# A transformer pair on one core: the first feed-forward and the second attention put on one clock of slots

## The reference, cut to what matters

```python
x = x + L0_attn(layernorm(x))   # 8 heads of 64, keys and values from a 64-wide latent
x = x + L0_ffn(layernorm(x))    # ternary weights, 256 -> 1024 -> 1024 -> 1024 -> 256
x = x + L1_attn(layernorm(x))   # 16 heads of 16, rotary, softmax over 1024 keys
x = x + L1_ffn(layernorm(x))    # integer weights, 256 -> 768 -> 256

# L0_ffn, t(x, w, s) = (x @ w.T) * s, w in {-1, 0, 1}
h = silu(t(x, w1, s1)) * t(x, w2, s2)
h = gelu(t(h, h1, hs1)); h = gelu(t(h, h2, hs2)); y = t(h, w3, s3)

# L1_attn
q, k = rope(x @ wq.T), rope(x @ wk.T)
p = softmax(q @ k.T / sqrt(16)); y = (p @ (x @ wv.T)) @ wo.T
```

## Time and profile before

| | us |
|---|---|
| median of the runs (2805.17 to 2809.58) | 2807.38 |
| the profiled execution's time | 2809.22 |
| its span, to which all rows belong | 2807.3 |
| TensorE busy in the span | 2590.9 |
| VectorE busy | 1782.3 |
| ScalarE busy | 1461.3 |
| GpSimd busy | 886.4 |

### The profile page before, as it was taken

One profiled execution on the slowest core, in us unless ns is written; L12 is line 12 of the kernel. 1 busy time (PEld: TensorE's weight loads), 2 busy tenths in 40 slices (PEclk: granted clock), 3 DMA queues, 4 the chain that ended last, 5 costly groups with the idle time before them and its releaser, 6 DMA issues. The chain is left out here.

```text
span 2807.3 us, 35409 instructions
## 1 busy us (share of the span) xinstructions
PE 2590.9 (92%) x13498; PEld 1661.5 (59%) x13498; DVE 1782.3 (63%) x2809; ACT 1461.3 (52%) x1936; POOL 886.4 (32%) x559
## 2 busy tenths in 40 slices
PE   6889889889897999999999949999999999999699
PEld 4444454445444878888888834555555555554488
DVE  6555555565554544555554458887887888787454
ACT  3343343443443446667666614666566566666443
POOL 1545546546554323444343321110010011000144
PEclk8999999999998999999999968999999999999899
DMA  1000000100004300000000043343333333231222
GB/s 52 9 13 22 27 24 23 32 24 24 16 24 126 106 1 23 23 23 23 23 19 5 16 113 68 64 88 59 69 65 58 74 80 62 52 54 18 88 83 76
DMA packets 118284, 129.77 MB, mean 46 GB/s; under 512 B 21216, under 2 KB 92384, under 8 KB 118112
## 3 DMA queue, kind: packets, MB, share of 16 engines
q1 hardware_dynamic: 118112, 127.46, 19.3%
HBM read 92.95 MB, written 33.68 MB: 45 GB/s over the span
## 5 line engine op out<-in xcount | busy, mean ns | idle before, releaser
L1945 DVE TENSOR_REDUCE c_mraw<-c_X 128x1 f32<-128x512 f32 x1024 | 651.3, 684 | 126.8 <-PE c_X L105 118.3
L1867 ACT ACTIVATE c_P<-c_S 128x1024 f32<-128x1024 f32 x512 | 495.8, 1020 | 245.9 <-PE c_S L105 242.2
L105 PE MATMUL c_X<-c_K,c_Q 96*128 96x512 f32 x1024 | 369.0, 443 | 13.4 <-DMA c_Q<-bounce_q 8.6
L488 ACT ACTIVATE a_P<-a_S 128x1024 f32<-128x1024 f32 x256 | 249.0, 1023 | 199.2 <-PE a_S L105 199.2
L105 PEld LDWEIGHTS c_X<-c_K,c_Q 96*128 96x128 f32 x1024 | 181.9, 193 | 267.5 <-issue 197.3
L604 DVE TENSOR_REDUCE a_mraw<-a_X 128x2 f32<-128x1024 f32 x168 | 205.4, 1222 | 147.1 <-PE a_X L105 147.1
L105 PE MATMUL c_S<-c_Q,c_K 98*128 98x512 f32 x1024 | 287.9, 403 | 2.0 <-DMA c_Q<-c_mrow 2.0
L105 PE MATMUL c_O<-c_P,c_V 128*32 128x512 f32 x2048 | 274.4, 608 | 0.2 <-ACT c_P L1867 0.2
L105 PE MATMUL a_O<-a_P,a_V 128*64 128x512 f32 x1024 | 264.2, 640 | 0.0
L1220 POOL TENSOR_TENSOR b_act0l<-b_xf,b_act0h 128x512 fp32r<-128x512 f32 x128 | 169.7, 1327 | 295.8 <-ACT b_act0h L1085 295.8
L733 POOL TENSOR_TENSOR a_accp<-a_accp,a_P 128x1024 f32<-128x1024 f32 x96 | 228.9, 2384 | 67.5 <-ACT a_P L488 58.0
(11 more groups left out here) (310 smaller groups left out, 5377.0 us busy)
## 6 DMA issues: line engine op xcount, KB each, us to landing
c_K<-bounce_k SPq DMA_DIRECT2D x64, 256.0 KB, 7.6
c_Q<-bounce_q SPq DMA_DIRECT2D x128, 128.0 KB, 4.5
b_h_w<-in_L_ffn_h_w SPq DMA_DIRECT2D x16, 512.0 KB, 7.4
bounce_k<-c_comp SPq DMA_DIRECT2D x16, 512.0 KB, 3.2
bounce_q<-c_comp SPq DMA_DIRECT2D x16, 512.0 KB, 3.0
a_rinv<-sums SPq DMA_DIRECT2D x62, 128.0 KB, 2.9
a_ln_x<-in_L_attn_x SPq DMA_DIRECT2D x8, 512.0 KB, 4.7
a_xres<-in_L_attn_x SPq DMA_DIRECT2D x32, 128.0 KB, 2.5
```

What stands on the lines that cost most here:

```text
L105: return pe.eng.matmul(out, lhsT, rhs, start=start, stop=stop, skip_group_check=True)
L488: act.eng.activation(P[n % NP][:, :, :], psS[n % 2][:, :, :], ACT.Exp, scale=SCALE).then_inc(s_exp)
L1867: act.eng.activation(P[n % NP][:, 2 * hp:2 * hp + 2, :], psS[hp][:, :, :], ACT.Exp, scale=SCALE).then_inc(s_exp)
L1945: dve.eng.tensor_reduce(mraw[u % 2][:, at:at + 1], psX[X.slot(key)][:, :], AX.X, ALU.max).then_inc(X.free(key))
```

## The change

`ffn_b` and `attention_c` are taken out and `ffn_attention` is put in their place, one stage of 722 slots (END = 192 + 512 + 18). Slots 0 to 511 are the eight blocks of the feed-forward, 64 slots each; from slot 192 on each slot also holds one half step of the attention (two heads, 128 keys), so that block k + 2 and later runs beside batch k/2. All engines walk through the same slots.

- TensorE in a slot: a pair of scores, a pair of maxima 24 half steps ahead, in even slots the weighing of four heads (two half steps), at most one piece of side work (`x_at`), then 3 products of the feed-forward in even slots and 8 in odd ones.
- Scores and maxima are pairs: two heads on rows 0 to 63 and 64 to 127, three products of halves in 48 rows, the maximum (one part, no longer two) in row 48. One reduction of 1024 columns replaces two of 512. V gets a 17th column of ones at a stride of 16 instead of 16 columns of ones.
- PSUM: one pair of banks for scores, one pair for maxima, one for O, one for all side work (X), two for the feed-forward (Y), where there had been eight for the feed-forward, and three for side work and maxima.
- Weights are not split: every tile is read again from HBM (`wcopy`, 512 KB each, a ring of three) and used as it is. Whether they are exact is found in `attention_a`: 22 times a tile is loaded, copied high by ScalarE, subtracted and reduced by VectorE, and copied from HBM to HBM. If they were not exact, the products would be made in float32.
- The feed-forward's Gelu is made twice by ScalarE, once into the high half and once into float32; before, a copy made the high half.
- Rotation is made by GpSimd in three instructions from a copy by ScalarE; VectorE only shuffles. Values go through HBM like q and k. Each key or query fetch is 6 DMAs instead of 4.
- The host lays out the weights as tiles, and the columns of wv in another order.

`attention_a` (in every unit u from 3 to 24: DMA in turn 2, ScalarE in turn 3, VectorE in turns 0 and 1 of the next unit):

```diff
+    LOWS, LOW_FIRST = 22, 10
+    def tile_at(u, j):
+        n, step = divmod(4 * u + j - LOW_FIRST, 4)
+        return (n, step) if 0 <= n < LOWS else None
 # sync
+            def load_tile(n):
+                sp.wait_ge(s_low, n)
+                sp.eng.dma_start(tile[:, :], wtiles[n]).then_inc(s_tile, 16)
+                sp.eng.dma_start(wcopy[n], wtiles[n]).then_inc(s_copy, 16)
 # scalar, last in a turn
+            def tile_high(n):
+                act.wait_ge(s_tile, 16 * (n + 1))
+                act.wait_ge(s_tile_lo, n)
+                act.eng.activation(tile_hi[:, :], tile[:, :], ACT.Copy).then_inc(s_tile_hi)
 # vector, last in a turn, behind add() and the norm's steps
+            def tile_low(n, step):
+                if step == 2:
+                    dve.wait_ge(s_tile_hi, n + 1)
+                    dve.eng.tensor_tensor(tile[:, :], tile[:, :], f32(tile_hi[:, :]), ALU.subtract).then_inc(s_tile_lo)
+                elif step == 3:
+                    dve.wait_ge(s_tile_lo, n + 1)
+                    dve.eng.tensor_reduce(lows[:, n:n + 1], tile[:, :], AX.X, ALU.max, apply_absolute_value=True).then_inc(s_low)
```

The new stage's clock and TensorE's program:

```diff
+    NB, MT, PER, SLOTS = 8, HID0 // 128, 22, 64
+    START, ML = 192, 24
+    BACK = (2, 4, 6, 8)
+    C_LOAD, C_STATS, C_SCALE, C_TURN = 10, 12, 13, (14, 16)
+    PROJECT = {18: ("k", 0), 22: ("q", 0), 26: ("k", 1), 30: ("q", 1)}
+    VALUES = {20: 0, 24: 1, 28: 2, 32: 3}
+    B_LOAD, B_STATS, B_SCALE, B_TURN = 34, 40, 42, (46, 50)
+    OUT_BACK = {52: 0, 53: 1, 56: 2, 59: 3, 69: 4, 74: 5, 75: 6, 79: 7}
+    OUT = {54: 0, 55: 1, 58: 2, 61: 3, 71: 4, 76: 5, 77: 6, 81: 7}
+    def slice_at(H):
+        k, s = divmod(H, SLOTS)
+        j = 11 * (s // 2)
+        return (k, *((j + 3, j + 11) if s % 2 else (j, j + 3))) if k < NB else (k, 0, 0)
 # tensor
+            def product(k, q, exact):
+                key, at, n = tile_of(k, q)
+                i = PER * k + q // 16
+                w, j, part = weights_of(i), at // 2, at % 2
+                if at == 0:
+                    pe.wait_free(Y, key)
+                    pe.wait_ge(s_w[i % 3], 16 * (i // 3 + 1))
...
+                ins = mm(pe, psY[Y.slot(key)][:, :], lhsT, rhs, at == 0, at == n - 1)
+            def maxima(k):
...
+                pe.wait_free(R, key)
+                for h in range(2):
+                    rows = slice(64 * h, 64 * h + 48)
+                    ins = mm(pe, pair(key)[:, h, :], QT[u % 3][rows, i, 128 * q:128 * q + 128], KT[u // 2 % 2][rows, i, 512 * kh:512 * kh + 512])
+                ins.then_inc(R.full(key))
+            def scores(h):
...
+                pe.wait_free(R, key)
+                for j in range(2):
+                    rows = slice(64 * j, 64 * j + 64)
+                    ins = mm(pe, pair(key)[:, j, :], KT[u // 2 % 2][rows, i, 128 * t:128 * t + 128], QT[u % 3][rows, i, :])
+                ins.then_inc(R.full(key))
+            def weigh(n):
...
+                for i in range(NH):
+                    ins = mm(pe, psO[32 * i:32 * i + 17, :], V[:, t, :, g * NH + i], P[(2 * n + i // 2) % 4][:, i % 2, :], t == 0, t == NT - 1)
+            def all_slots(exact):
+                for H in range(END):
+                    if half_step(H) is not None:
+                        scores(half_step(H))
+                    if maximum_at(H) is not None:
+                        maxima(maximum_at(H))
+                    if weigh_at(H) is not None:
+                        weigh(weigh_at(H))
...
+                    if x_at(H):
+                        side(x_at(H))
+                    k, lo, hi = slice_at(H)
+                    for q in range(lo, hi):
+                        product(k, q, exact)
```

The order of the other engines in a slot, and what leaves the two banks Y:

```diff
 # scalar
+            for H in range(END):
+                if half_step(H) is not None:
+                    exponent(half_step(H))
...
+                for key in ended_at(H - 1):
+                    if key[0] == "up":
+                        gate_high(key)
+                if send_high_at(H):
+                    send_high(*send_high_at(H)[1:])
+                for key in ended_at(H):
+                    if key[0] != "up":
+                        leave(key)
+            def leave(key):
...
+                elif key[0] == "hidden":
+                    (dst, m), scale = into(key), scol[:, 2 + key[2], key[3]:key[3] + 1]
+                    act.wait_ge(s_lo, fs(key) - 1)
+                    act.eng.activation(act_buf[dst][0][:, m, :], bank[:, :], ACT.Gelu, scale=scale).then_inc(s_hi)
+                    act.eng.activation(xf[fs(key) % 2][:, :], bank[:, :], ACT.Gelu, scale=scale).then_inc(Y.free(key))
 # vector
+            for H in range(END):
+                if maximum_at(H) is not None:
+                    reduce(maximum_at(H))
...
+                for key in ended_at(H):
+                    if key[0] == "up":
+                        up(key)
+                if norm_at(H):
+                    norm_step(*norm_at(H))
 # gpsimd
+            def rotate(kk, what, j):
...
+                pool.eng.tensor_tensor(t1[:, :], qk[:, :], rope[:, 0, :], ALU.mult).then_inc(s_rot)
+                pool.wait_ge(*X.emptied(("project", kk, what, j)))
+                pool.eng.tensor_tensor(t2[:, :], t2[:, :], rope[:, 1, :], ALU.mult).then_inc(s_rot)
+                pool.wait_ge(s_rot, 3 * i + 2)
+                pool.eng.tensor_tensor(t1[:, :], t1[:, :], t2[:, :], ALU.add).then_inc(s_rot)
 # sync
+            def load_weights(i):
+                if i >= 3:
+                    sp.wait_ge(*Y.filled(last_of(i - 3)))
+                sp.eng.dma_start(f32(wt[i % 3][:, :]), wcopy[i % PER]).then_inc(s_w[i % 3], 16)
```

More of the change, by code:

```diff
@@ L213, in turn_dve, with attention_a @@
                               ALU.subtract).then_inc(self.ring.free(key))
-def attention_a(nc, x_in, x_out, weights, c_ident, scratch):
+def attention_a(nc, x_in, x_out, weights, c_ident, scratch, wtiles, wcopy, inexact):
     NH, NG, NP, AHEAD = 2, 4, 6, 6
@@ L289, in x_order @@
             out += [("sums", sums_at(u, j))] if sums_at(u, j) is not None else []
+            out += [("low",)] if judge_at(u, j) == 1 else []
         return out + [("sums", NU - 1)] + [("out", b, t) for b, t in TAIL]
@@ L323, in attention_a @@
         xres = [p.sb(f"xres{i}", [128, 256]) for i in range(4)]
+        tile, tile_hi = p.sb("tile", [128, 1024]), p.sb("tile_hi", [128, 1024], F32R)
+        lows, low_all, low_top = p.sb("lows", [128, LOWS]), p.sb("low_all", [128, 1]), p.sb("low_top", [1, 1])
+        s_copy, s_tile, s_tile_hi, s_tile_lo, s_low = p.sem("copy"), p.sem("tile"), p.sem("tile_hi"), p.sem("tile_lo"), p.sem("low")
         s_ident, s_identr, s_fill = p.sem("ident"), p.sem("identr"), p.sem("fill")
@@ L560, in scalar @@
                     norm.scale_act(act, norm_at(u, j)[0], 4 * half, 4 * half + 4)
+                if tile_at(u, j) and tile_at(u, j)[1] == 1:
+                    tile_high(tile_at(u, j)[0])
             keep_out(NU - 1)
@@ L695, in vector @@
                     norm_step(*norm_at(u, j))
+                if tile_at(u, j):
+                    tile_low(*tile_at(u, j))
+                if judge_at(u, j) is not None:
+                    judge(judge_at(u, j))
             add(STEPS - 1)
@@ L925, in tensor @@
                     sums(sums_at(u, j))
+                if judge_at(u, j) == 1:
+                    pe.wait_free(X, ("low",))
+                    pe.wait_ge(s_low, LOWS + 1)
+                    pe.eng.transpose(bank(("low",))[0:1, 0:128], low_all[:, :], ident[:, :]).then_inc(X.full(("low",)))
             for n in (STEPS - 2, STEPS - 1):
@@ L2216, in shape_constants, with weight_tiles @@
     return {"c_ident": np.eye(128, dtype=np.float32), "c_rope": rope}
+TILED = tuple(f"L0_ffn_{n}" for n in ("w1_w", "w2_w", "h1_w", "h2_w", "w3_w"))
+def weight_tiles(w1, w2, h1, h2, w3):
+    rows = [np.asarray(w).T.reshape(-1, 128, w.shape[0]).transpose(1, 0, 2) for w in (w1, w2, h1, h2, w3)]
+    tiles = [np.stack([w[:, :, 256 * q:256 * q + 256] for w in rows[:2]], 1) for q in range(4)]
+    tiles += [w[:, :, 128 * m:128 * m + 128] for w in rows[2:] for m in range(w.shape[2] // 128)]
+    return np.ascontiguousarray(np.stack([t.reshape(128, 1024) for t in tiles]).astype(np.float32))
 def lay_out(inputs):
@@ L2230, in lay_out @@
             arrays[n] = np.ascontiguousarray(a.reshape(-1, 128).T)
+    arrays["L0_ffn_tiles"] = weight_tiles(*(inputs[n] for n in TILED))
     arrays.update(shape_constants())
```

1514 lines of the change are left out of this document (633 added, 881 removed).

## The result

The changed kernel takes 2942.1 us (median of 2940.6 and 2943.6), 1.0487 of the time before (95% interval 1.0470 to 1.0504). The forecast was 2763, range 2660 to 2880: wrong, and outside the range. The profiled execution has a span of 2941.8 us.

The account below looks back on a forecast made before the run. TensorE was taken to bound both merged stages. The terms 891.6 + 45 + 305 + 957 + 388 + 3 (barrier) + 173.6 gave 2763 us, 1.6% below the time before, range 2660 to 2880.

Parts of the forecast that it names:

- What bounds: Feed-forward and second attention: TensorE busy 708 of 731 and 900 of 914 us, so it bounds both merged stages.
- First attention: 22 weight-tile checks added: 31 us of exposed subtractions plus 14 of slower clock, sum 45, from 10 to 86.
- Start and feed-forward alone: Merged stage's start and slots 0 to 191: 305 us, with 14 us before the first product.
- my three terms of matmuls: Slots 0 to 191: products 239 us, side work 23, maxima with two switches of tiling 15.
- Both together: Slots 192 to 511, feed-forward beside attention: 2.99 us a slot, 957 us, with VectorE and ScalarE below that.
- The tail: Slots 512 to 721, attention alone: single buffer bounds, reductions 1.83 us apart, 388 us, or 391 with the barrier.
- that rival: Slots after 512: TensorE's clock falls to half, 2840 to 2917 us in all; chance 0.11.
- One sign of mine: After slot 512: reductions of 1024 columns every 1.9 us, with TensorE near 60% busy.
- Everything overlaps: Slots 192 to 511 at 2.75 us each, first attention +20, 2661 us in all; chance 0.25.
- Pairs of 48 rows: Paired score and maximum matmuls run concurrently, 0.23 us a pair; the rival that they do not, 2876 us, chance 0.05.
- The drain at a change of tiling: Slots 192 to 511: five tiling changes per two slots cost 0.80 us; without them the sum is 2635.
- Single buffers bite: Slots 192 to 511 at 3.3 us through waits for X, Y or a pair, 2862 us; chance 0.14.

Follow-up runs that it names:

- the runs above: Changed kernel with Tanh for the merged stage's Silu and Gelu, 2746.9 us; with Tanh for the gates' Silu only, 2879.0 us.
- 240 stand-ins of 1.42 us: Changed kernel, Tanh for Silu and Gelu, two unused 128x640 Copies per would-be table switch: 2918.3 us ahead of the tile wait, 3018.1 with Silu's and Gelu's behind.

## Why the prediction was wrong, step by step

*What bounds.* "TensorE bounds both stages that are merged" was read rightly, and from it I went on as if it would bound their union. It does only without the loads (99% busy).

*First attention, right.* 45 against 47.8 (39 to 48 over the six profiles with this code). Both parts of the term showed: the subtraction exposed in front of the reduction, and the slower weighing behind the longer wait (3.50 us). Its waits for the maxima between 77 and 870 us grew by 26 (97.6 us against 71.7 before), and its busy time by 19 (799.1 against 779.7) at a clock of 0.94 for 0.96. I had 31 and 14: the mechanism was right, but that the sum is so near is luck, two misses of 5 us that cancel. The subtraction took 1.22 us and not the 1.40 that I read from one into fp32r (22 x 1.22 = 27), and the clock cost more.

*Start and feed-forward alone, 20 short.* TensorE starts 17.3 us in, not 14. In the rest it is idle 12.9 us (308.2 less 295.3), about the 14 that I charged, but for other causes (the 4.4 us of "issue" lie ahead of this stretch):

```profile
L105 PE MATMUL m_Y<-m_ln_hi,m_wt 128*128 128x512 f32 x98 | 43.1, 439 | 6.2 <-issue 4.4 <-ACT m_gate L1458 1.6
L105 PE MATMUL m_R<-m_K,m_Q 48*128 48x512 f32 x50 | 12.7, 505 | 4.2 <-DMA m_Q<-bounce_q 4.2
L193 PE MATMUL m_X<-m_ident,m_ln_x 128*128 128x128 f32 x40 | 7.3, 312 | 6.2 <-DVE m_ln_x L173 6.2
```

The gates' chain, which I gave 8, is 1.6; the norm's scale and a fetch of queries are 10. The miss is in the busy time: 295 where my three terms of matmuls made 277 (239 + 23 + 15). It is in the products: from start to start, waits left out, the side work took the 23 that I gave it and the maxima with their changes of tiling about the 15, but the products 257 where I had 239. Most take 0.23 us from their start to the next, but some 38 of the 1056 take 0.42 to 0.59, about what the lower level of the clock makes of 0.23 (8 us in all; the stretch's clock is 0.97), and another 60, with no change of tiling beside them, 0.31 to 0.37 (6 us). My price of 0.227 came from an unbroken run of products, and it holds neither kind.

*Both together: the step that failed.* It is the sentence "VectorE (1.22 + 0.4) and ScalarE (1.02 + 0.7) stay below". The 0.7 counted the ACTIVATEs of the feed-forward and not what must stand between an exp and a Gelu: 239 switches, 0.75 a slot, of 1.40 us. ScalarE was to get 1.72 us a slot and got 2.66, in lumps of 3.9 us ahead of an exp where a tile ends. At the 0.75 us of end time that a switch cost in the runs above this is 180 us, and 957 + 180 = 1137 is 2% from the 1113.7. All else in this step stood: 5.24 against 5.21 for two slots, and 2.92 against 2.99 with side work and stalls (the stalls were the smaller part: TensorE idles 0.04 us a slot there, where I charged 0.10).

*The tail, right.* 388.1 against 391. The clock granted there is 0.96 (0.98 up to the last maxima, 0.84 in the 65 us behind them), so that rival falls; the rhythm is that of the single buffer as worked out: the median distance of two reductions is 1.82 us, for my 1.83 (135 of 168 lie between 1.75 and 1.85). One of the longer, beside side work:

```profile
2500.53 1.23 DVE L1515 TENSOR_REDUCE m_mraw<-m_R 128x2 f32<-128x1024 f32 x1 [0.24 <-PE m_R L105]
...
2502.52 1.23 DVE L1515 TENSOR_REDUCE m_mraw<-m_R 128x2 f32<-128x1024 f32 x1 [0.20 <-PE m_R L105]
```

One sign of mine did not come: TensorE is busy 79% of the tail (308 of 388 us) and not near 60%. My 2.1 of 3.8 us counted bare slots by distances of starts and left out the side work; the time did not hang on it.

*The rivals.* *Everything overlaps* needed 2.75 a slot; even without loads it is 2.92. Pairs of 48 rows run beside each other (0.33 us for two of 512 columns with the change of tiling). The drain at a change of tiling held too: without it the two slots would be 4.41 us, and they are 5.24. *Single buffers bite* named 3.3 a slot and the right symptom, TensorE waiting for the pair buffer, but not the cause: with the same buffers and no loads there is nothing to wait for. The buffers only make the loads hurt.

What was open when I predicted was not the price, 1283 ns in a row of before, but the question: which operations of the two streams cannot stand next to each other for nothing.

## What to carry to other kernels

When two stages are interleaved, count for ScalarE not only the instructions of both but the alternations between their table sets: here 1.4 us of ScalarE for each, and about 0.75 us of the end time, since part of it falls into time in which ScalarE would have been idle. If the finer grain is wanted, bring both streams into one set first: functions written out with Tanh, Square and Copy cost far less than the loads did. And a new instruction on an engine in order belongs in the turn where that engine is not the one waited for; the same subtraction and reduction cost some 34 us more in one turn than in the next.

## What the hardware showed that I had not expected

- A switch of tables held ScalarE for 1.40 us: 1.28 for the load and 0.1 for the overlap of neighbouring ACTIVATEs that it prevents. No longer drain is in the rows.
- A load runs ahead of the wait for the tile that the ACTIVATE behind it reads (43 of 120 started before the tile's last product did), so it can hide in idle time. 240 stand-ins of 1.42 us cost 166 us ahead of the waits and 268 with half of them behind.
- TensorE's waits cost it twice: 135 us idle and 44.5 us of slower matmuls, at a granted clock of 0.96 (most of the time at 2.4 GHz, some at 1.2) against 1.00. Behind a wait of 1.81 us a weighing took 1.92 us instead of 1.07.
